# A two-layer-normed attention and expert block on one core: full-array products gathered into two places of a step, VectorE's and ScalarE's work reordered, and the last batch's experts shared out differently

## The reference, cut to what matters

```
mod = silu(c) @ wmod                           # six rows of 128: shift, scale and gate, twice
h = layernorm(x) * (1 + ca) + sa
q, k, v = h @ Wqkv + bqkv                      # 16 heads of width 8
K = exp(-|q - k|^2 * sigma)                    # no softmax: nothing is normalised
x = x + ga * ((K @ v) @ Wproj + bproj)
h = layernorm(x) * (1 + cb) + sb
mask = the two largest of h @ w_router + b_router, as 0 and 1, of 8 experts
x = x + gb * sum_e mask_e * (h @ w_e + b_e)    # all 8 experts are computed
```

## Time and profile before

| | us |
|---|---|
| median of 3 executions | 229.1 (227.3 to 229.19) |
| the profiled execution | 230.45 |
| its span, first to last instruction | 228.4 |

### The profile page before, as it was taken

One profiled execution on the slowest core, in us unless ns is written; L12 is line 12 of the kernel. 1 busy time (PEld: TensorE's weight loads), 2 busy tenths in 40 slices (PEclk: granted clock), 3 DMA queues, 4 the chain that ended last, 5 costly groups with the idle time before them and its releaser, 6 DMA issues.

```text
span 228.4 us, 8135 instructions
## 1 busy us (share of the span) xinstructions
PE 211.7 (93%) x3230; PEld 149.2 (65%) x3230; DVE 166.0 (73%) x589; ACT 169.8 (74%) x254; POOL 141.9 (62%) x207
## 2 busy tenths in 40 slices
PE   7788987999999999999999999999899999999780
PEld 6464544576777776767767776776676767676580
DVE  6894536277877778777868687878678777868685
ACT  3217888888888888878787988888788878767160
POOL 6725564565858585857677595858385856305465
PEclk9967999999999999999999999999999999999996
DMA  6462323231434342432325133424342323300001
GB/s 164 128 199 83 132 78 120 87 118 61 152 75 146 90 147 90 143 89 93 123 76 164 61 119 98 139 69 153 80 145 70 141 69 104 108 1 26 23 3 46
DMA packets 22471, 22.93 MB, mean 100 GB/s; under 512 B 2330, under 2 KB 20258, under 8 KB 22434
## 3 DMA queue, kind: packets, MB, share of 16 engines
q1 hardware_dynamic: 21962, 21.79, 29.6%
q10 hardware_dynamic: 472, 0.62, 0.8%
HBM read 6.65 MB, written 2.12 MB: 38 GB/s over the span
## 4 chain that ended last, share of the span: by engine, by line
PE 73%; POOL 5%; DMA 5%; ACT 5%; DVE 4%; SPq 4%; issue 3%; POOLq 0%; DVEq 0%
PE att_ps L911 22%; PE scores L893 10%; PE ffn_ps L1025 7%; PE qkv_ps L926 7%; DMA st<-norm_parts 5%; PE ffn_ps L1026 5%; PE ffn_ps L1027 5%; PE mid_ps L969 2%; ACT probs L490 2%; PE qkv_ps L956 2%; PE qkv_ps L935 2%; PE mid_ps L1002 2%; POOL hl L406 2%; SPq L316 2%; PE scores L840 2%
## 5 line engine op out<-in xcount | busy, mean ns | idle before, releaser
L490 ACT ACTIVATE probs<-scores 128x1024 f32<-128x1024 f32 x128 | 124.0, 1022 | 20.6 <-PE scores L893 20.6
L911 PE MATMUL att_ps<-probs,vpad 128*32 128x256 f32 x1024 | 68.5, 385 | 0.0
L682 DVE SCALAR_TENSOR_TENSOR acc<-ffn_ps,mask,acc 128x128 f32<-128x128 f32 x218 | 61.3, 343 | 9.6 <-PE ffn_ps L1027 9.5
L893 PE MATMUL scores<-st 32*128 32x256 f32 x512 | 37.3, 331 | 4.3 <-DMA st<-norm_parts 2.6
L911 PEld LDWEIGHTS att_ps<-probs,vpad 128*32 128x32 f32 x1024 | 26.7, 109 | 19.6
L361 POOL TENSOR_TENSOR ve<-stats,eps 128x2 f32<-128x2 f32 x32 | 6.2, 195 | 51.5 <-DVE stats L662 51.5
L1025 PE MATMUL ffn_ps<-we_hi,h_hi 128*128 128x256 f32 x110 | 35.7, 325 | 0.6 <-POOL h_lo L423 0.6
L893 PEld LDWEIGHTS scores<-st 32*128 32x128 f32 x512 | 23.5, 185 | 13.1 <-issue 3.3
L1026 PE MATMUL ffn_ps<-we_hi,h_lo 128*128 128x256 f32 x110 | 30.7, 279 | 0.0
L1027 PE MATMUL ffn_ps<-we_lo,h_hi 128*128 128x256 f32 x110 | 30.6, 278 | 0.0
L404 POOL TENSOR_TENSOR sq<-qkf 128x512 f32<-128x512 f32 x15 | 15.6, 1042 | 19.6 <-DVE qkf L688 19.6
(11 more groups left out here) (146 smaller groups left out, 332.2 us busy)
## 6 DMA issues: line engine op xcount, KB each, us to landing
st<-hl SPq DMA_DIRECT2D x47, 256.0 KB
rb_all<-rb_rows SPq DMA_DIRECT2D x16, 192.0 KB, 3.4
out_dram<-x_all SPq DMA_DIRECT2D x16, 128.0 KB, 3.1
x_all<-in_L_attn_x_dram SPq DMA_DIRECT2D x13, 128.0 KB, 3.3
st<-norm_parts SPq DMA_DIRECT2D x60, 16.0 KB
we_sb<-in_L_ffn_w_experts_dram SPq DMA_DIRECT2D x1, 512.0 KB, 5.3
w_mod_sb<-in_L_wmod_dram SPq DMA_DIRECT2D x1, 256.0 KB, 4.4
st<-hl ACTq DMA_DIRECT2D x1, 256.0 KB
```

The costliest lines, as they stand in the source:

```text
L490: nc.scalar.activation(probs[:, g, 2 * half:2 * half + 2, :], scores[:, 2 * half:2 * half + 2, :], ACT.Exp, scale=two_sigma).then_inc((exp ...
L682: v.scalar_tensor_tensor(acc[:, q, t, :], y, m, acc[:, q, t, :], ALU.mult, ALU.add).then_inc(acc_step, 1)
L893: i = pe.matmul(scores[:, r, t * T:(t + 1) * T], st[rows, par, g, t * P:(t + 1) * P], st[rows, par, g, T:2 * T], start=True, stop=True)
L911: i = pe.matmul(att_ps[r * ROWS:(r + 1) * ROWS, 0:T], heads[:, g * ROWS:(g + 1) * ROWS], probs[:, g, r, t * T:(t + 1) * T], start=(g == 0 ...
```

## The change

Nothing is computed differently but for sums of the end; order, engines and banks move.

- TensorE's step: quarters 2 and 3 of batch k-3 now follow each other behind `qk_scores(k, 1)`, quarters 0 and 1 of batch k-2 stand at the end of the step around the two turns, and between these places are only strips, the mask's turn and the bias rows. `pv(k-1, 2)`'s second half and `pv(k-1, 3)` run in step k; `router` moves one step on. The four quarters use the banks `qkv_ps`, `ffn_ps`, `att_ps`, `ffn_ps`; `turn_x` writes `mid_ps`.
- VectorE takes the high parts and the mask's rows from ScalarE, and `choose`, `split_h2` and the adds of the experts stand elsewhere in its step.
- At the end ScalarE multiplies quarters 2 and 3 of the last batch by the mask as well, and TensorE adds these four products to the bias rows with the identity (`last_sum`). `last_experts` makes quarters 0 to 2 of the last batch in two passes, first what needs the high part only. GpSimd no longer handles the last batch's bias; it takes batch 14's products first.
- At the start one preset of `st` is done by ScalarE, GpSimd's presets wait for the first norm rows, idle matmuls (`warm_up`) are placed differently, and four of them (`fill`) are gone.

```diff
-        bias_sb_ok = sem("bias_sb_ok")
-        bias_res = sem("bias_res")
-        last_gated = sem("last_gated")
+        last_ps = sem("last_ps")
+        last_step = sem("last_step")
+        last_ok = sem("last_ok")
         def has(b):
             return 0 <= b < NB
         def f_bank(b, c):
+            if b <= NB - 4:
...
                 par = k % 2
-                if has(k + 2) and k != 0:
+                if k < 0:
                     rsqrt(0, k + 2, par, bn1, ve1, rstd1)
-                    if k == -2:
-                        preset(0, 1)
                     if k == -1:
                         normalise(k + 2, par)
+                        pool.wait_ge(norm_ok, 1)
                         preset(1, 0)
                         preset(1, 1)
                         nc.gpsimd.memset(vpad[:, 1, :, :, :].rearrange("p t h w -> p (t h w)"), 0.0).then_inc(vpad1_ok, 1)
...
+            def products(b, c):
+                p = EC * (c - NC // 2) + NE // 2 * (b - NB + 2)
+                act.wait_ge(f_ps, NC * b + c + 1)
+                for e in range(EC):
+                    for t in range(NT):
+                        i = nc.scalar.mul(prod[:, p + e, t, :], f_bank(b, c)[:, (t * EC + e) * C:(t * EC + e + 1) * C],
+                                          mask[:, b % 2, t, 0, EC * c + e:EC * c + e + 1].bitcast(F32))
+                    i.then_inc(prod_ok, 1)
...
@@ -688,6 +712,12 @@
                 v.tensor_tensor(qkf[:, :, :], qkv_ps[:, :].rearrange("p (a n) -> p a n", a=2),
                                 bqk_col[:, :].unsqueeze(2).broadcast_to([P, 2, T]), ALU.add).then_inc(qkf_ok, 1)
+            def high_parts(b):
+                dve.wait_ge(st_in[(b - 1) % 2], stacked(b - 1))
...
                     gate_rows()
                     expert_weights(0)
                     queries_keys(1)
                     expert_weights(1)
+                    return
+                if k == -2:
+                    return
+                if has(k - 2):
+                    choose(k - 2)
+                if has(k + 1):
+                    if k > 0:
+                        queries_keys(k + 1)
+                    high_parts(k + 1)
+                if has(k - 3):
+                    experts(k - 3, 2)
+                if has(k - 1):
+                    first_residual(k - 1)
+                if has(k + 1):
+                    norm_rows(k + 1)
+                if has(k - 1):
+                    second_stats(k - 1)
+                if has(k + 2):
+                    first_stats(k + 2)
+                if has(k - 2):
+                    mask_rows(k - 2)
...
-                                ALU.mult).then_inc(last_gated, 1)
-                dve.wait_ge(last_gated, 1)
-                dve.wait_ge(bias_res, 1)
-                v.tensor_tensor(x_all[:, b, :], x_all[:, b, :], acc[:, par, :, :].rearrange("p t c -> p (t c)"), ALU.add).then_inc(res_ok, 1)
+                                ALU.mult).then_inc(last_step, 1)
+                dve.wait_ge(last_step, 2)
+                v.tensor_tensor(x_all[:, b, :], x_all[:, b, :], wide, ALU.add).then_inc(last_ok, 1)
             dve.wait_ge(ident_ok, 1)
             columns()
             v.memset(vpad[:, 0, :, :, :].rearrange("p t h w -> p (t h w)"), 0.0).then_inc(vpad_ok, 1)
...
                             pe.wait_ge(o_ok, b)
+                            if 3 <= b < NB - 1:
...
                 pe.wait_ge(xn_ok, b + 1)
-                if b > 0:
+                if b == 1:
...
+                if b < NB - 2:
+                    pe.wait_ge(x1_ok, b + 2)
...
+            def last_sum():
+                for e in range(NE // 2):
+                    pe.wait_ge(prod_ok, NE // 2 + e + 1)
+                    i = pe.matmul(b_bank(NB - 1), ident[:, :], prod[:, NE // 2 + e, :, :].rearrange("p t c -> p (t c)"),
+                                  start=False, stop=e == NE // 2 - 1)
+                i.then_inc(last_ps, 1)
...
+                if b <= NB - 4 and c == 0:
+                    pe.wait_ge(v_ok, b + 4)
+                elif b <= NB - 4 and c == 2 and b < NB - 4:
+                    pe.wait_ge(o_ok, b + 3)
+                elif b <= NB - 4 and c == 1:
+                    if b > 0:
+                        pe.wait_ge(acc_step, steps(b, 0))
+                elif b <= NB - 3:
                     pe.wait_ge(acc_step, steps(b, (c - 1) * EC * NT))
                 elif b == NB - 2 and c == 0:
                     pe.wait_ge(acc_step, steps(b - 1, 3 * EC * NT))
-                elif b == NB - 1 and c != 1:
-                    pe.wait_ge(acc_step, (steps(b - 2, STEPS), 0, steps(b - 1, EC * NT), steps(b - 1, 2 * EC * NT))[c])
-                elif b < NB - 2 and NC * b + c > 0:
-                    pe.wait_ge(acc_step, EC * NT * (NC * b + c))
+                elif b == NB - 1 and c == 3:
+                    pe.wait_ge(prod_ok, EC)
...
             def start():
                 qk_rows(0)
                 values(0)
+                warm_up(2)
                 norms(0)
                 more_modulation()
+                warm_up(2)
...
+                qk_scores(k, 0)
+                if has(k - 1):
+                    pv(k - 1, 2, (1,))
+                if has(k - 2):
+                    router(k - 2)
                 if has(k - 1):
                     pv(k - 1, 3)
-                if has(k + 1) and k >= 0:
+                if has(k + 1):
                     qk_rows(k + 1)
-                if k == 0:
-                    fill(4)
+                qk_scores(k, 1)
+                if has(k - 3):
+                    experts(k - 3, 2)
+                    experts(k - 3, 3)
+                if has(k - 1):
+                    project(k - 1)
+                if has(k + 1):
+                    norms(k + 1)
+                qk_scores(k, 2)
                 if has(k - 2):
                     turn_mask(k - 2)
-                if has(k - 3):
-                    experts(k - 3, 3)
+                pv(k, 0)
+                if has(k + 1):
+                    values(k + 1)
+                pv(k, 1)
                 if has(k - 2):
                     expert_bias(k - 2)
-                if k == NB - 1:
+                qk_scores(k, 3)
+                pv(k, 2, (0,))
+                if has(k - 2):
                     experts(k - 2, 0)
-                if has(k):
-                    qk_scores(k, 1)
-                    pv(k, 0, (0,))
-                if has(k - 1):
-                    project(k - 1)
-                if has(k + 1) and k >= 0:
-                    norms(k + 1)
-                if has(k - 2):
-                    experts(k - 2, 0 if k < NB - 1 else 1)
-                if has(k):
-                    qk_scores(k, 2)
-                    pv(k, 0, (1,))
-                    pv(k, 1, (0,))
-                if has(k + 1) and k >= 0:
-                    values(k + 1)
-                if has(k - 2):
-                    experts(k - 2, 1 if k < NB - 1 else 2)
                 if has(k - 1):
                     turn_x2(k - 1)
-                if has(k):
-                    qk_scores(k, 3)
-                    pv(k, 1, (1,))
-                    pv(k, 2)
-                if has(k - 1):
-                    router(k - 1)
                 if has(k + 2):
                     turn_x(k + 2)
-                if k == -2:
-                    warm_up(1)
                 if has(k - 2):
-                    experts(k - 2, 2 if k < NB - 1 else 3)
+                    experts(k - 2, 1)
```

285 lines of the change are left out of this document (180 added, 105 removed).

## The result

The changed kernel takes **233.84 us** (median of 4 executions, 231.77 to 237.2) against 229.14 of the kernel before beside it (227.3 to 230.79): ratio **1.0205, interval 1.013 to 1.028**. It is slower; 227.7 was forecast. Three of the four executions had a granted clock under 0.99. In two later comparisons on other chips, 12 executions each, the ratio was 1.0079 (1.0033 to 1.0126) and 1.0082 (1.0031 to 1.0132), with medians of 231.48 against 228.87 and 232.23 against 228.62.

A forecast was written before the change was run, and what follows sets the result against it. TensorE was taken to bound the full steps. 0 + 1.3 - 0.9 - 0.3 - 1.5 = -1.4 took the profiled 230.45 to 229.05; that profile lay 1.35 above its median, hence 227.7 us, range 223.2 to 231.8.

The forecast's parts named there:

- start, to step 2: Start up to step 2: shorter low rows of batch 0 and no `fill` bring the stack of batch 1 earlier, -0.9 us.
- step 2: The step behind the start: six expert products fewer, which come back at the end, -0.3 us.
- end: Last batches: statistics and last output no longer behind GpSimd's gate and chain, -1.5 us, between 0 and -2.5.
- the high rows: VectorE's full step: it takes their copy from ScalarE, where it took 0.62, at between 0.39 and 0.78 us.
- the 0 for a full step: Twelve full steps: -0.14 of TensorE shape changes and up to +0.3 of waiting taken as 0, between -0.14 and +0.15.
- adds nothing if it takes under 1.04: Stack of batch k+1: GpSimd's squares set the low rows' start, so VectorE's copy of the high rows costs nothing below 1.04.
- late for quarter 0: Late in a full step: VectorE's values' bias done at 10.2, 0.3 us after TensorE wants it for quarter 0.
- the full array's shapes: TensorE's full step: changes of shape cost 0.93 instead of 1.07 us, 0.14 less.
- Rival A: TensorE's full steps: row strips to whole array and whole array to columns are free, 0.30 less a step, 224.1 us, chance 0.26.
- The stack: Stack of batch k+1: last issue 0.6 later, quiet steps stay covered, two others pay 0.6 each, +1.3 us.
- rival B: Full steps: the stack becomes the bound once a quiet landing takes over 2.65, +5.4, 231.8 us, chance 0.18.
- rival D: Start: without `fill` TensorE's clock stays low longer, first scores and rows take twice as long, +1.5, 229.2 us, chance 0.06.

The follow-up runs named there:

- the fastest kernel: the mended kernel with the stack's third large DMA issued by ScalarE from step 2 on only: 225.56 us, ratio 0.9879.
- the mended kernel: changed kernel; GpSimd's squares wait for VectorE's cast from step 2, 22 idle products in steps 0 to 2, last gate waits for VectorE's normalising: 228.10 us, ratio 0.9952.

## Why the prediction was wrong

The span's sum, from the two profiled executions (230.0 - 228.4 = +1.6; forecast -1.4):

| step | forecast | profile |
|---|---|---|
| twelve full steps, with the stack | 0 + 1.3 | +2.7 |
| start, to step 2 | -0.9 | -2.4 |
| step 2 | -0.3 | +1.9 |
| end | -1.5 | -0.6 |

**The step that failed: the high rows "on VectorE between 0.39, a copy of half the size, and 0.78", and with it the 0 for a full step, which took 0.3 more (12.40 against 12.10).** The price came from a half-size copy that had itself a GpSimd instruction beside it when it started, and I did not ask what that costs:

```profile
110.84 0.39 DVE L729 CAST h_hi<-h 128x256 fp32r<-128x256 f32 x1
110.35 0.74 POOL L378 TENSOR_TENSOR x_all<-x_all,gated 128x256 f32<-128x256 f32 x1
```

In the profile after, where no GpSimd instruction wider than two columns runs beside it, the same copy (L765) takes 0.28 to 0.29. I then wrote that the copy of the high rows "adds nothing if it takes under 1.04" and that GpSimd's squares would be slower. It was VectorE that stood: 1.30 in every full step, 0.5 above my upper bound, while the squares kept their 1.04. Both engines are released by the same `qkf`, so they meet in every step. The change had moved the cast from ScalarE, which took 0.62 (104.02) beside those same squares (104.06), to the engine that GpSimd holds up.

**And the wrong place to look.** I asked whether VectorE's values would be late for quarter 0 (0.3). No such wait exists in the profile after. I had the first residual at 5.75 into the step; it came at 6.06 (119.69 - 113.63), and at 5.62 with the squares later (68.94 - 63.32). But the mask's turn, which writes the bank that this residual reads, comes only 0.9 us behind the norms. It was no term of my sum and no rival. The chain from `qkf` through the cast to the residual to the mask's turn is where 0.36 of each step went.

**Right in direction, and in part by luck: the full array's shapes.** I had 0.14 less a step. Free of the wait, the steps take 12.04 against 12.10: 0.06 less. Row strips to the whole array I took at 0.22; the eight scores took their usual 0.43 (116.50 to 116.93) and only the first product was longer by 0.11. Whole array to columns, taken at 0.08, was 0.09 (118.33 to 118.54, 0.21 against 0.12). Columns to row strips, taken at 0.08, was 0.11 (119.00 to 119.33 less 0.22). By these prices 0.2 should have gone. Part of the rest is two costs that I had not counted: in a quiet step of the fastest kernel the mask's turn, now followed by column strips, takes 0.21 (116.39 to 116.60) instead of 0.12, and the sixteen of the projection 0.55 (115.04 to 115.59) instead of 0.44. Rival A, which had this entry and this exit free, fell: neither is. The rule of the Trainium skill, TensorEngine Tiling, Key Properties, that any change of mode drains the engine, fits the exits, and the entry's 0.11 too; against it, eight scores ahead of column strips took no more than elsewhere (0.44, 106.90 to 107.34).

**The stack** (forecast +1.3, of which two steps at 0.6 are 1.2; rival B +5.4): it did not bind in the changed kernel, whose longer steps cover it. In the twelve full steps TensorE's matmuls never waited for it in that profile, its weight loads once, for 0.3. It binds as soon as steps are 12.04: the twelve then took 1.7 to 4.4 more than 12 x 12.04 in the five profiles in which SyncE issues all seven. Rival B named the right resource and the wrong condition. A quiet landing does not bind at 2.65, since scores have started 1.8 behind the last issue; what costs is that now and then an issue in SyncE's line of seven is long, and now and then a landing is late.

**The start**: up to step 2 it gave 2.4 instead of 0.9; with the presets alone in the old kernel it was 0.8 by the first scores and 2.3 by step 2, so they are nearly all of it. **The clock** (my rival D, 0.06, +1.5) came not at the start but at step 2, behind 3.2 us of gaps that began with step 1. It cost 1.6 in the profile, and 13 of the 28 executions had a clock below 0.99, about as many as of the kernel before. Of the distance from 227.7 to 233.84, 2.7 are the profile's and 3.4 are that the profile of before lay 1.35 above its median and that of after 2.07 below its own. I had carried the first over and could not know of the second. The other two chips put the median at 231.5 and 232.2, inside the range or just above it.

**The end** gave 0.6 of 1.5. The other 0.9 is less than the 1.1 that the normalising lost beside the gate and that came back with one wait (29.42 to 28.35).

## What to carry to other kernels

Before an instruction such as this cast moves to VectorE, look what GpSimd does at that moment: if one event releases both, allow for the neighbour's duration plus its own (1.04 + 0.43 here, 1.30 measured), not for a row of other company. Ask of every instruction that the late engine frees, its banks included, not only of those it feeds. And a gain in the steady steps is worth what the next limit leaves: here 0.36 a step bought 0.2 us in the mean until the gaps of the first steps were filled, and 3.5 together with that.

## What the runs showed of the hardware that I had not expected

- VectorE's copy of 128x512 from SBUF to SBUF took 0.43 us alone and 1.30 beside a GpSimd product of 1.04 that had started 0.03 earlier; two 128x128 operations with a scalar took 0.60 and 1.72. GpSimd's own instruction of 1.04 took 1.04 with and without VectorE beside it.
- Some DMA issues of SyncE take 1.2 to 2.0 us instead of 0.3 to 0.7: 8 of 130 between 36 and 200 us of the kernel before, each repeated some 61 us later where the time allows it. Why, the runs do not show; with an issue of every step moved to ScalarE's queue, they still came.
- Where the scores waited for the stack behind a long issue, they started 1.8 to 2.2 us after the start of its last small DMA's issue; in a few steps that DMA took 3.5 to 3.8 to land, with nothing different in its issue.
- TensorE's granted clock fell to its lower level at some 38.5 us, behind gaps of 0.9, 0.8 and 1.5 us between 29 and 37.5. With twenty-two idle products in those gaps it was at 0.99 or more over the kernel in 12 executions of 12, 10 of 12, 6 of 12, 4 of 6 and 5 of 6, in the five kernels that have them; in the changed kernel in 15 of 28. They help and do not settle it.
- Within the same clock and kernel, spans still differ by 2 us (at 0.997 to 1.0 the mended kernel had 223.4, 223.9, 225.5 and 226.0). Late landings are a guess; this is not shown.
